# Layer-0 attention of a perceiver kernel: where ACT takes the exponentials, and where PE projects the value tiles

## The reference, cut to what matters

```python
q = (query @ Wq + bq).reshape(B, Nq, H, D).transpose(0, 2, 1, 3)
k = (key_value @ Wk + bk).reshape(B, Nkv, H, D).transpose(0, 2, 1, 3)
v = (key_value @ Wv + bv).reshape(B, Nkv, H, D).transpose(0, 2, 1, 3)
attn = jnp.einsum('bhqd,bhkd->bhqk', q, k) * scale
attn = jnp.clip(attn, -CLAMP, CLAMP)
attn = jax.nn.softmax(attn, axis=-1)
x = jnp.einsum('bhqk,bhkd->bqhd', attn, v).reshape(B, Nq, Cq)
return x @ Wo + bo
```

## Time and profile before

| | |
|---|---|
| median of three runs | 1053.65 us (1051.8 to 1057.92) |
| profiled execution | 1050.78 us, of which the span of the profile is 1048.9 us |
| mean granted TensorE clock | 0.892 |
| PE busy | 873.1 us (83%), weight loads 656.7 us |
| DVE busy | 644.3 us (61%) |
| ACT busy | 424.4 us (40%) |
| POOL busy | 216.5 us (21%) |
| largest DVE group, L892 (maxima) | 448 operations, 253.1 us |
| largest ACT group, L668 (exponentials) | 196 operations, 190.3 us |

### The profile page before, as it was taken

One profiled execution on the slowest core, in us unless ns is written; L12 is line 12 of the kernel. 1 busy time (PEld: TensorE's weight loads), 2 busy tenths in 40 slices (PEclk: granted clock), 3 DMA queues, 4 the chain that ended last, 5 costly groups with the idle time before them and its releaser, 6 DMA issues. The chain is left out here.

```text
span 1048.9 us, 21226 instructions
## 1 busy us (share of the span) xinstructions
PE 873.1 (83%) x7297; PEld 656.7 (63%) x7299; DVE 644.3 (61%) x1116; ACT 424.4 (40%) x575; POOL 216.5 (21%) x234
## 2 busy tenths in 40 slices
PE   4989998989988989989989716699599999997604
PEld 3577676666766766766766505565388887886403
DVE  4855745745746646647557212489477777786792
ACT  2255565565555655655654702210023333332001
POOL 4432202202102102012020290223012223220000
PEclk9588999998999998989999955799799999998765
DMA  5963553553543644637514120320000000000000
GB/s 174 222 149 88 115 149 88 116 144 76 141 132 84 145 120 96 145 94 202 146 52 95 70 93 0 116 71 11 1 13 16 17 17 17 17 17 1 1 0 5
DMA packets 44151, 85.35 MB, mean 81 GB/s; under 512 B 11647, under 2 KB 26944, under 8 KB 42176
## 3 DMA queue, kind: packets, MB, share of 16 engines
q1 hardware_dynamic: 44110, 84.87, 31.4%
HBM read 45.27 MB, written 0.25 MB: 43 GB/s over the span
## 5 line engine op out<-in xcount | busy, mean ns | idle before, releaser
L892 DVE TENSOR_REDUCE cu<-ps 128x1 f32<-128x448 f32 x448 | 253.1, 618 | 68.5 <-PE ps L1322 65.7
L668 ACT ACTIVATE pr<-ps 128x1024 f32<-128x1024 f32 x196 | 190.3, 1026 | 2.5 <-PE ps L1404 1.3
L433 POOL TENSOR_TENSOR pause<-pause 128x1 f32<-128x1 f32 x41 | 13.0, 317 | 650.8 <-DVE mr L904 441.3
L1322 PE MATMUL ps<-khl,qp 32*128 32x448 f32 x448 | 135.6, 482 | 3.3 <-DVE cu L892 0.6
L1404 PE MATMUL ps<-qs,ks 128*128 128x256 f32 x784 | 128.4, 300 | 11.3 <-ACT pr L668 7.7
L1416 PE MATMUL ps<-pr,v 128*17 128x128 f32 x3136 | 113.1, 286 | 25.5 <-ACT pr L668 25.0
L1404 PEld LDWEIGHTS ps<-qs,ks 128*128 128x128 f32 x784 | 103.9, 190 | 34.2 <-issue 17.5
L1416 PEld LDWEIGHTS ps<-pr,v 128*17 128x17 f32 x3136 | 78.7, 100 | 53.6 <-issue 31.0
L1571 PE MATMUL ps<-ks,ct 128*128 128x512 f32 x352 | 99.4, 404 | 2.7 <-ACT ks L762 2.3
L1322 PEld LDWEIGHTS ps<-khl,qp 32*128 32x128 f32 x448 | 59.6, 187 | 63.0 <-DVE cu L892 25.9
L620 ACT COPY v<-ps 128x256 f32<-128x256 f32 x98 | 36.6, 373 | 143.9 <-PE ps L1312 143.9
(11 more groups left out here) (262 smaller groups left out, 1129.3 us busy)
## 6 DMA issues: line engine op xcount, KB each, us to landing
ks<-khl SPq DMA_DIRECT2D x168, 224.0 KB, 5.2
nm<-maxima SPq DMA_DIRECT2D x14, 1024.0 KB, 4.6
raw<-in_ctxT SPq DMA_DIRECT2D x14, 448.0 KB, 3.8
raw<-in_ctxT SPq DMA_DIRECT2D x28, 224.0 KB, 4.3
ffw<-in_mask_q SPq DMA_DIRECT2D x1, 1568.0 KB, 10.6
raw<-in_ctxT SPq DMA_DIRECT2D x12, 128.0 KB, 2.2
raw<-in_ctxT SPq DMA_DIRECT2D x22, 64.0 KB, 1.8
raw<-in_ctxT SPq DMA_DIRECT2D x44, 32.0 KB, 2.0
```

Source lines behind the costliest of these rows:

```text
L668: nc.scalar.activation(pr[:, (HALVES * b + u) % 4, :], bank(2 * (u % 2), 2), ACT.Exp).then_inc(S["e0_exp"], 1)
L892: V.tensor_reduce(cu2[:, h, half:half + 1], ps[:, use_bank(n), 0:NB], AX_X, ALU.max).then_inc(S["e0_red"], 1)
L1322: mm(ps[:, use_bank(n), 0:NB], qp[part, t, e, :], khl[part, 0, t, half * NB:(half + 1) * NB], start=True, stop=True).then_inc(S["e0_head"], 1)
```

## The change

The list of PE's order is rewritten. Step 0 now holds 7 coarse units and V0 to V3, in two pairs; steps 1 to 5 are all alike, scores, three units, weighing, two units; step 6 begins with the weighing and takes R0 and R1, then V4 to V6, R2, R3 and L as before. All counts are the same (32 units, 7 value tiles); the number of places stays a multiple of three.

On ACT, the exponentials of tile t+1 are issued where `S` stands in step t: in step 0 between the evictions of K1 and K2, in steps 1 to 5 first and alone. Both halves of the context cast come at the end of step 0. In step 6, `S` brings `fall_spread` and the exponentials of tile 0 of the next chunk. On DVE the branch on the clip flag moves to the place of `S`, and the flag is read at `L`.

```diff
--- before.py
+++ after.py
@@ -73,10 +73,9 @@
 
 
 
-LIST = [["K0", "F", "K1", "S", "K2", "K3", "W", "m", "m"]]
-LIST += [["S", f"V{t}", "m", "m", "m", "W", "m", "m", "m"] for t in range(4)]
-LIST += [["S", "m", "m", "m", "W", "m", "m", "m", "R0", "R1"],
-         ["W", "V4", "V5", "V6", "R2", "R3", "L", "", "", "S"]]
+LIST = [["K0", "F", "K1", "S", "K2", "K3", "W", "m", "m", "m", "V0", "V1", "m", "m", "V2", "V3", "m", "m"]]
+LIST += [["S", "m", "m", "m", "W", "m", "m"]] * 5
+LIST += [["W", "R0", "R1", "V4", "V5", "V6", "R2", "R3", "L", "", "", "S"]]
 UNITS = 2 * H
 
 
@@ -657,25 +656,35 @@
                 max_row(0, i)
             fall_spread(0)
 
+            def exponentials(c, b, t):
+
+                for u in (2 * t, 2 * t + 1):
+                    g = HALVES * c + u
+                    act.wait_ge(S["e0_ok"], g + 1)
+                    act.wait_ge(S["e0_score"], g + 29)
+                    act.wait_ge(S["e0_pv"], g + 11)
+                    nc.scalar.activation(pr[:, (HALVES * b + u) % 4, :], bank(2 * (u % 2), 2), ACT.Exp
+                                         ).then_inc(S["e0_exp"], 1)
+
+            exponentials(0, 0, 0)
+
             def chunk0(c, b, i2, nxt=True, split=True, sums=False):
 
                 for t in range(TPC):
-                    for u in (2 * t, 2 * t + 1):
-                        g = HALVES * c + u
-                        act.wait_ge(S["e0_ok"], g + 1)
-                        act.wait_ge(S["e0_score"], g + 29)
-                        act.wait_ge(S["e0_pv"], g + 11)
-                        nc.scalar.activation(pr[:, (HALVES * b + u) % 4, :], bank(2 * (u % 2), 2), ACT.Exp
-                                             ).then_inc(S["e0_exp"], 1)
-                    if nxt and t == 0:
-                        act.wait_ge(S[f"e0_keys{b}"], 192 * (i2 + 1))
-                        act.wait_ge(S["e0_head"], UNITS * (c + 1))
                     for kind, i, n in STEPS[t]:
-                        if kind == "F":
+                        if kind == "S" and t < TPC - 1:
+                            exponentials(c, b, t + 1)
+                        elif kind == "F":
                             factor_copy(c)
                         elif not nxt:
                             continue
+                        elif kind == "S":
+                            fall_spread(c + 1)
+                            exponentials(c + 1, 1 - b, 0)
                         elif kind == "K":
+                            if i == 0:
+                                act.wait_ge(S[f"e0_keys{b}"], 192 * (i2 + 1))
+                                act.wait_ge(S["e0_head"], UNITS * (c + 1))
                             key_block_hi(c + 1, i)
                         elif kind == "V":
                             if i == 0:
@@ -686,10 +695,8 @@
                                 act.wait_ge(S["e0_score"], HALVES * (c + 1) + 27 + i // 2)
                                 act.wait_ge(S["e0_row_out"], 16 * (c + 1))
                             max_row(c + 1, i)
-                    if split and t in (2, 3):
-                        split_hi0(c + 2, b, t - 2)
-                    if nxt and t == TPC - 1:
-                        fall_spread(c + 1)
+                    if split and t == 0:
+                        split_hi0(c + 2, b)
                     if sums and t in (1, 2):
                         k = t - 1
                         act.wait_ge(S["ld_ffw"], 32)
@@ -935,10 +942,15 @@
                 dve.sem_inc(S["carried_clip"], 1)
                 return dve.value_load(clipf[0:1, 0:1], min_val=0, max_val=1)
 
-            def prepare(c, b, t):
+            def prepare(c, b, t, flag):
 
                 for kind, i, n in STEPS[t]:
-                    if kind == "K":
+                    if kind == "S" and (t < TPC - 1 or c < NCH):
+                        clip(c - 1 + (t + 1) // TPC, (t + 1) % TPC, flag)
+                    elif c == NCH:
+                        if kind == "K" and i == 1:
+                            rescale(c - 1)
+                    elif kind == "K":
                         key_block_lo(c, i)
                         if i == 1 and c > 0:
                             rescale(c - 1)
@@ -949,6 +961,13 @@
                         if i == UNITS - 1:
                             half_maxima(c, b, 1)
                             after_maxima(c, b)
+                    elif kind == "L":
+                        flag = clip_flag(c)
+                        with dve.If(flag < 1):
+                            dve.sem_inc(S["e0_ok"], HALVES)
+                            dve.sem_inc(S["clip_min"], HALVES)
+                            dve.sem_inc(S["clip_max"], HALVES)
+                return flag
 
             def rescale(c):
 
@@ -956,7 +975,7 @@
                 dve.wait_ge(S["e0_pv"], HALVES * c + 14)
                 V.tensor_tensor(ps[:, 4, :], ps[:, 4, :], fs, ALU.mult).then_inc(S["e0_scaled"], 1)
 
-            def clip(c, u):
+            def clip_half(c, u):
 
                 k, z = HALVES * c + u, u % 2
                 s = bank(2 * z, 2)
@@ -971,22 +990,17 @@
                 dve.wait_ge(S["clip_max"], k + 1)
                 dve.sem_inc(S["e0_ok"], 1)
 
-            for t in range(TPC):
-                prepare(0, 0, t)
-            for c in range(NCH):
-                flag = clip_flag(c)
-                with dve.If(flag < 1):
-                    dve.sem_inc(S["e0_ok"], HALVES)
-                    dve.sem_inc(S["clip_min"], HALVES)
-                    dve.sem_inc(S["clip_max"], HALVES)
+            def clip(c, t, flag):
+
+                if flag is not None:
+                    with dve.If(flag > 0):
+                        clip_half(c, 2 * t)
+                        clip_half(c, 2 * t + 1)
+
+            flag = None
+            for c in range(-1, NCH):
                 for t in range(TPC):
-                    with dve.If(flag > 0):
-                        clip(c, 2 * t)
-                        clip(c, 2 * t + 1)
-                    if c + 1 < NCH:
-                        prepare(c + 1, (c + 1) % 2, t)
-                    elif t == 0:
-                        rescale(c)
+                    flag = prepare(c + 1, (c + 1) % 2, t, flag)
                 if c == 1:
                     dve.wait_ge(S["mask_halved"], 5)
                     words = mflat4[:, :].rearrange("p (u w) -> p u w", w=UNIT // 4)
```

## The result

| | before | after |
|---|---|---|
| median of three runs | 1053.65 us | 981.70 us (980.14 to 982.61) |
| ratio, 95% interval | | 0.931 (0.926 to 0.936) |
| span of the profile | 1048.9 us | 979.9 us |
| mean granted clock | 0.892 | 0.915 |
| copy of R3, chunk 0 | 55.42 us | 59.11 us |

The kernel is 72 us faster where 53 were forecast. In the profiles the periods give 13 x 5.55 = 72.1 us, the start of the stage takes 3.7 back, and the rest is 0.6 shorter, together the 69.0 by which the spans differ. From chunk 13 to the end the profiles of this document take 467.9 to 472.9 us, so the 0.6 means nothing, and medians that lie 2 or 3 us apart say little by themselves.

The account below looks back on a forecast made before the run. PE's order of work was taken to set the period, with a hole where PE and ACT wait on each other. 12.4 + 17.45 + 6.0 = 35.85 us against 40.17, 4.1 saved after allowance, times 13: 53 us, so 1000 us; range 990 to 1023.

Parts of the forecast that it names:

- The hole: PE idle between steps 5 and 6, waiting for ACT's exponentials of tile 6; about 2.1 us a period to be saved.
- The clock: Granted clock of 0.63 behind the hole, in step 6; full clock after the change saves 1.74 us a period.
- 0.5 units and value tiles that mesh better: Rest of the 4.3 us saved a period, beside about 2.1 for the hole and 1.7 for the clock.
- allowance: 0.2 us a period taken off the saving for small waits not placed (the branch, the loop's jump).
- 0.77 + 0.58: Steps 1 to 5: PE's time in us for three units and for two units, within a step of 3.49.
- 2.85 us of 3.49: Steps 1 to 5: DVE's five maxima against the step's length, plus at most 0.2 us for the branch.
- Ahead of the stage DVE's 32 maxima still set the pace: nothing.: Start, before chunk 0: no time gained or lost there.
- the 2.9 us that the forecast put on top: Profiled execution before was 2.9 us below the median shown, so 997 became a predicted 1000.
- Chunk 13 and what follows: End of the kernel: nothing gained in chunk 13, and what follows moves as a whole.
- The rival of the clock that still falls: Step 6 or step 0: the 1.74 us isn't given back, 2.4 us a period saved, 1022 us; 17%.
- DVE becomes the bound: Steps: maxima and branch at 3.7 us, or exponentials waited for; saved 2.6 to 3.0 a period, 1014 to 1020 us; 13%.

Follow-up runs that it names:

- hole_back: r_early with, on ACT, the exponentials of tile 6 again behind the copies of R0 and R1; 1031.42 us, 38.59 us a period.
- r_early: Kernel after with R0 and R1 back at the end of step 5, ahead of the weighing of tile 6; 985.69 us, 35.10 us a period.
- fill: Kernel before with 8 matmuls of zeros on PE ahead of the weighing of tile 6; 1032.77 us, 38.72 us a period.
- half_max_before: Kernel before with each DVE maximum taken over half of its 448 columns; 1037.06 us, 38.88 us a period.
- calm_start: Kernel after with DVE's first row of maxima set ahead of the query work and POOL's mask halving held until DVE has the first chunk's maxima; 972.50 us.
- swap: Kernel after with two units behind the scores and three behind the weighing in steps 1 to 5; 973.24 us, 34.42 us a period.
- list_only: Kernel before with only the new list of PE's order, old code on ACT and DVE; 1006.43 us, 36.87 us a period.

## Why the prediction was wrong

**Direction, mechanism, clock: right.** The hole was ACT's order at tile 6; it costs 2.28 us (2.1 forecast; hole_back at full clock against r_early). The clock fell because of it: 1.45 (fill) or 1.2 us (hole_back), 1.74 forecast from a single period that is short by some 0.2 us for another reason. Together they are 3.5 us by hole_back, 3.8 forecast. Both go in the changed kernel.

**The step that failed: "0.5 units and value tiles that mesh better".** Take the 3.5 us off the 5.55, and 2.0 are left for PE's order, four times the term. It was no term that I had reasoned about; it was what remained of the sum. The mechanism of the steps was wrong as well: the sum let PE alone set them, with room on DVE, where a ring through DVE and PE does. Part by part, against the trace after:

| part | forecast | measured |
|---|---|---|
| K0 to the first unit | 7.12 | 7.10 |
| V0, V2 behind K0 | 8.35, 10.33 | 8.35, 10.27 |
| step 0 | 12.4 | 12.1 |
| one of steps 1 to 5 | 3.49 | 3.27, 3.25, 3.25, 3.47, 3.25 |
| steps 1 to 5 | 17.45 | 16.5 |
| step 6 | 6.0 | 5.9 |
| allowance | 0.2 | none |
| period | 36.05 | 34.62 |

Two thirds of the 1.43 us are in steps 1 to 5, and there in the units: 0.77 + 0.58 were charged, and 0.57 + 0.54 measured in step 5 (226.79 to 227.36, 228.36 to 228.90). The 0.77 came from a group in which PE had waited for DVE, and I took the interval from one group to the next as PE's cost. half_max_before showed it: 0.40 us without the wait. Having charged a wait as work, I then checked DVE against the step so made, found 2.85 us of 3.49, and took that for room; the true order is the reverse, since PE's own step is 2.94 and the ring through DVE makes it 3.25. Two errors of opposite sign left 0.24 a step: PE's part was charged 0.55 too high, and 0.31 for the ring was missing. That they cancel in part is luck. The same overcharge at the last pair of step 0 (0.58 for 0.40) is most of the 0.3 there.

**The start.** "Ahead of the stage DVE's 32 maxima still set the pace: nothing." That missed the two collisions of DVE with POOL: one the profile of before has too (2.86 us for 8 columns), the other only that of after, 3.7 us later at R3's copy. With neither, in calm_start, that copy comes at 52.60, 2.8 earlier than before. In swap, with the second alone, it comes at 53.15. The second collision does cost swap some 3 us (7.1 from the operation on 8 columns to R3's copy, 4.05 in calm_start), but swap gets there 2.5 us earlier: its first maximum comes at 26.55 and not 27.81 (its cast took 0.43 us, in calm_start 2.18), and DVE waits 1.25 us less for PE among the maxima, where the clock is 1.00 from 28 to 31 us and in calm_start 0.62. Why the clock differs there stays open.

**The whole miss.** The forecast of 997 us for the profiled execution, less 13 x 1.43 = 18.6 and 0.6 behind the stage, plus 3.7 at its start, makes 981.5; 981.70 was measured. It was the median of its three, so the 2.9 us that the forecast put on top, to 1000, had no counterpart.

**The rest.** Chunk 13 and what follows moved as a whole, within the scatter. The 0.2 for small waits had no counterpart. The rival of the clock that still falls, with the rule of the Trainium skill's "TensorE: Matmul & The Clock Gate" (section "A second HAM failure mode: psum-queue depth-cycling"), is out here: step 0 has weight loads idle for 0.56 and 0.35 us at banks, and its clock is 1.00. But list_only shows how near it was: with a wait of 1.3 us more, for ACT's exponentials, the clock fell in 6 of the 12 later periods. "DVE becomes the bound" was right as to the engine and wrong as to the price. The range ended at 990 because its low end let a step fall from 3.49 to 3.4 us and no further, though the 3.49 held a wait of 0.37.

## What to carry to other kernels

The interval between two groups of a pipelined engine is its cost only if nothing in it was a wait; take the shortest instance in the trace, or one with no idle time in brackets, and look for the waits inside a group too. Where an engine is last in line for a copy, put it right behind what feeds it: a wait of 2 us of TensorE cost 3.5 with the clock. Two engines that each idle can still bind each other through a short ring of buffers; add up the ring once round before calling either one free.

## What the runs showed of the hardware that I had not expected

- Eight matmuls of zeros in a hole of 2.4 us kept the granted clock at 1.00 in the last 12 of 13 periods and made the kernel 2.0% faster.
- With waits of 1.3 and 0.4 us in each period beside the shorter ones, the clock fell in 6 of the last 12 periods (list_only); with waits of 0.2 to 0.6 us alone, several in each period, in none of the last 12 of the kernel after. The first period starts at a low clock in both.
- POOL's fill of 6.1 us stretched a DVE operation on 16 columns to 5.2 us (0.18 in calm_start, with nothing beside it), and POOL's halving of the mask one on 8 columns to 3.3 us (0.17 in calm_start); DVE's maxima over PSUM, 0.54 us apart, were not disturbed by POOL at all.
